# Query halves turned by a DMA instead of by TensorE in a two-layer attention kernel

## The reference, cut to what matters

```python
def l2norm(t):
    n = jnp.maximum(jnp.linalg.norm(t, axis=-1, keepdims=True), 1e-12)
    return t / n
x = x + _L0_cond_ref(x, mask_BxS_bf1, ...)
x = x + _L1_cond_ref(x, fside_16xSxS_0, mask_BxS_bk0, ...)
x = x + _L2_cond_ref(x, cond_64, ...)
x = x + _L3_cond_ref(x, cond_64, ...)
```

## Time and profile before

| | us |
|---|---|
| median of 3 runs | 1609.54 (1609.19 to 1610.14) |
| the profiled execution, its own time | 1607.64 |
| its span, first to last instruction | 1605.8 |
| the two attention layers, from the first bias step (40.5) to the last (1261.5) | 1221 |
| behind them, nearly all expert layers | 344.3 |
| mean granted TensorE clock, share of full speed | 0.988 |

### The profile page before, as it was taken

How to read it: one execution, slowest core, us unless ns; L and a number is a source line. 1 busy time by engine, 2 the same in 40 slices (tenths; PEclk the granted TensorE clock), 3 DMA queues, 4 the chain that set the end, 5 groups by cost and what they waited for, 6 DMA issues and landing times.

```text
span 1605.8 us, 45604 instructions
## 1 busy us (share of the span) xinstructions
PE 1435.0 (89%) x15700; PEld 1077.4 (67%) x15700; DVE 1394.6 (87%) x3629; ACT 1154.0 (72%) x3061; POOL 901.5 (56%) x1766
## 2 busy tenths in 40 slices
PE   4777878888999999977789999999999999999998
PEld 3555656666777777755666777777878656666665
DVE  6667888899999999977789999999999889888887
ACT  4666778888989999977788888889889633333332
POOL 6676778775756556577665354444343366622222
PEclk9899999999999999999999999999999999999999
DMA  5002211112222133012222122333333100000000
GB/s 159 18 30 72 67 48 54 62 66 74 80 87 86 55 107 118 23 48 67 54 61 80 61 74 87 97 97 107 113 116 94 38 27 21 1 1 1 14 14 27
DMA packets 67362, 100.70 MB, mean 63 GB/s; under 512 B 20330, under 2 KB 43968, under 8 KB 67136
## 3 DMA queue, kind: packets, MB, share of 16 engines
q1 hardware_dynamic: 65828, 97.12, 19.1%
q10 hardware_dynamic: 1308, 0.67, 0.2%
HBM read 91.41 MB, written 2.17 MB: 58 GB/s over the span
## 4 chain that ended last, share of the span: by engine, by line
PE 56%; DVE 22%; issue 7%; ACT 6%; POOL 4%; DVEq 0%; ACTq 0%; POOLq 0%
PE tp L1833 9%; DVE biased L1289 6%; PE sc L1696 6%; DVE p_lo L1387 6%; PE sc L1481 4%; PE sc L1483 4%; PE sc L1482 4%; PE sc L1697 4%; DVE q_a L1321 3%; PE aux L1481 3%; PE op L1481 3%; PE aux L1483 2%; PE aux L1482 2%; PE op L1483 2%; PE op L1482 2%
## 5 line engine op out<-in xcount | busy, mean ns | idle before, releaser
L1387 DVE TENSOR_TENSOR p_lo<-tp,p_hi 128x256 f16<-128x256 f32 (+3 forms) x896 | 422.0, 495 | 73.7 <-ACT p_hi L968 65.4
L1833 PE MATMUL tp<-ident,probs 128*128 128x128 f32 x2304 | 416.6, 281 | 18.7 <-DVE p_lo L1387 16.9
L968 ACT ACTIVATE p_hi<-tp 128x256 f16<-128x256 f32 (+3 forms) x896 | 384.9, 445 | 40.5 <-PE tp L1833 25.5
L868 ACT ACTIVATE probs<-biased,neg_max 128x256 f32<-128x256 f32 (+7 forms) x512 | 395.8, 773 | 17.5 <-DVE neg_max L1289 16.2
L1481 PE MATMUL op<-v_s,p_hi 128*128 128x64 f16 x2304 | 297.2, 194 | 23.7 <-DVE p_lo L1387 15.0
L1696 PE MATMUL sc<-k_a,q_a 128*128 128x512 f16 (+3 forms) x768 | 253.6, 330 | 69.0 <-DVE neg_max L1289 54.1
L1833 PEld LDWEIGHTS tp<-ident,probs 128*128 128x128 f32 x2304 | 262.7, 142 | 56.2 <-DVE p_lo L1387 44.3
L1482 PE MATMUL op<-v_s,p_hi 128*128 128x64 f16 x2304 | 296.9, 193 | 0.0
L1483 PE MATMUL op<-v_s,p_lo 128*128 128x64 f16 x2304 | 296.9, 193 | 0.0
L1481 PEld LDWEIGHTS op<-v_s,p_hi 128*128 128x128 f16 x2304 | 220.0, 99 | 41.5 <-DVE p_lo L1387 25.2
L1697 PE MATMUL sc<-k_b,q_b 128*128 128x512 f16 (+3 forms) x768 | 241.3, 328 | 0.0
(11 more groups left out here) (356 smaller groups left out, 3612.5 us busy)
## 6 DMA issues: line engine op xcount, KB each, us to landing
bias<-rel_table SPq DMA_DIRECT2D x4, 2048.0 KB, 9.1
bias<-in_fside_16xSxS SPq DMA_DIRECT2D x4, 2048.0 KB, 9.0
bias<-rel_table SPq DMA_DIRECT2D x4, 1792.0 KB, 7.3
bias<-in_fside_16xSxS SPq DMA_DIRECT2D x4, 1792.0 KB, 7.9
bias<-rel_table SPq DMA_DIRECT2D x4, 1536.0 KB, 6.1
bias<-in_fside_16xSxS SPq DMA_DIRECT2D x4, 1536.0 KB, 7.0
bias<-rel_table SPq DMA_DIRECT2D x4, 1280.0 KB, 5.9
bias<-in_fside_16xSxS SPq DMA_DIRECT2D x4, 1280.0 KB, 6.5
```

The lines of the kernel that those rows point to most:

```text
L868: ac.activation(probs[:, i % 2, 0:w], biased[:, i % 2, 0:w], ACT.Exp, bias=neg_max[:, u % 2, i % HU:i % HU + 1], scale=-1.0, accum_out=row ...
L968: ac.activation(p_hi[:, gi % 4, 0:nb * P], tp[gi % 2][:, 0:nb * P], ACT.Copy)\
L1387: ve.tensor_tensor(p_lo[:, gi % 4, 0:nb * P], tp[gi % 2][:, 0:nb * P], p_hi[:, gi % 4, 0:nb * P], ALU.subtract).then_inc(s["p_lo"], 1)
L1833: last = te.transpose(tp[gi % 2][:, jj * P:(jj + 1) * P], probs[:, n % 2, (j0 + jj) * P:(j0 + jj + 1) * P], ident[:, :])
```

## The change: queries rounded first, turned by a DMA

Queries of all 128 units are rounded to two fp16 halves while still in row layout, stored side by side per head (`q_16`: head, half, 64 numbers), and one DMA transpose per unit writes both halves, stacked on 128 partitions, into `q_a`. GpSimd's copy now goes from `q_a` to `q_b`. TensorE's two transposes, ScalarE's two copies and VectorE's two subtractions of k=3 are gone. In layer 0 the rounding stands behind the norm, at k=0 of the slot group two units ahead: ScalarE copies `q_n` from SBUF, VectorE subtracts from SBUF. In layer 1 it stands at k=1, from PSUM, in place of the copy to `q_n`. `q_n` has one buffer now. `queries_by_dma` is true for every unit, so the old branches stay in the code unused. In the diff below the two ScalarE pieces are the slots k=0 (layer 0) and k=1 (layer 1), then VectorE's, then TensorE's behind the projection.

```diff
+        q_16 = sb("q_16", [P, 2, HU, 2, DH], F16)
+        def queries_by_dma(u):
+            return u >= 0
...
+        def turn_queries(eng, u):
+            if not (u < NU and queries_by_dma(u)):
+                return
+            eng.wait_ge(s["q_low"], query_turns(u))
+            if u >= 2:
+                eng.wait_ge(s["scores"], HU * (u - 1))
+            eng.dma_start_transpose(q_a[:, u % 2, :].rearrange("p (h q) -> p h q", q=P),
+                                    q_16[:, u % 2, :, :, :].rearrange("p h e d -> p (h e d)")).then_inc(s_queries[u % 2], 16)
...
             load_bias(sp, 1)
+            turn_queries(sp, 0)
+            turn_queries(sp, 1)
             n_jobs = 3
             for g in range(2, STEPS * HG):
                 if g % HG == 0 and g <= 3 * HG:
                     write_table(sp, g // HG)
-                for u in (2 * g - 5, 2 * g - 4):
-                    turn_outputs(sp, u)
+                turn_queries(sp, 2 * g - 2)
+                turn_outputs(sp, 2 * g - 5)
+                turn_queries(sp, 2 * g - 1)
+                turn_outputs(sp, 2 * g - 4)
                 load_bias(sp, g)
-                if n_jobs < 10 and g == load_at(n_jobs) + 1:
+                if n_jobs < 10 and g == load_at(n_jobs) + (4 if n_jobs == 5 else 1):
...
             def query_copy(u):
+                if queries_by_dma(u):
+                    pool.wait_ge(s_queries[u % 2], 16 * pair_turns(u))
+                    gp.tensor_copy(q_b[0:DH, u % 2, :], q_a[0:DH, u % 2, :]).then_inc(s["q_dup"], 1)
...
+                if k == 0 and 0 <= m + 2 < U0:
+                    u = m + 2
+                    act.wait_ge(s["q_nd"], u + 1)
+                    if u >= 2:
+                        act.wait_ge(s_queries[u % 2], 16 * pair_turns(u - 2))
+                    ac.activation(q_16[:, u % 2, :, 0, :], q_n[:, 0, :].rearrange("p (h d) -> p h d", h=HU),
+                                  ACT.Copy).then_inc(s["q_high"], 1)
...
+                        ac.activation(q_16[:, u % 2, :, 0, :], first[:, 0:UW].rearrange("p (h d) -> p h d", h=HU),
+                                      ACT.Copy, scale=DH ** -0.5 / WS).then_inc(s["q_high"], 1)
...
+                if k == 1 and U0 <= m + 3 < NU:
+                    u = m + 3
+                    dve.wait_ge(s["q_high"], query_turns(u))
+                    ve.scalar_tensor_tensor(q_16[:, u % 2, :, 1, :], first[:, 0:UW].rearrange("p (h d) -> p h d", h=HU),
+                                            DH ** -0.5 / WS, q_16[:, u % 2, :, 0, :], ALU.mult, ALU.subtract)\
+                        .then_inc(s["q_low"], 1)
+                if k == 0 and 0 <= m + 2 < U0:
+                    u = m + 2
+                    dve.wait_ge(s["q_high"], query_turns(u))
+                    ve.tensor_tensor(q_16[:, u % 2, :, 1, :], q_n[:, 0, :].rearrange("p (h d) -> p h d", h=HU),
+                                     q_16[:, u % 2, :, 0, :], ALU.subtract).then_inc(s["q_low"], 1)
...
+                    if u < U0:
+                        take(False, (s["q_na"], u + 1), (s["q_sq"], u + 1))
+                    else:
+                        take(False, (s["q_high"], query_turns(u)), (s["q_low"], query_turns(u)))
```

More of the change, by code:

```diff
@@ L124, in model @@
         q_b = sb("q_b", [P, 2, HU * P], F16)
-        q_n = sb("q_n", [P, 2, UW])
+        q_n = sb("q_n", [P, 1, UW])
+        q_16 = sb("q_16", [P, 2, HU, 2, DH], F16)
         q_sq = sb("q_sq", [P, HU, DH])
@@ L247, in halves_first, with query_turns, pair_turns @@
             return u // UNITS % TILES >= TILES // 2
+        def queries_by_dma(u):
+            return u >= 0
+        def query_turns(u):
+            return sum(queries_by_dma(i) for i in range(u + 1))
+        def pair_turns(u):
+            return sum(queries_by_dma(i) for i in range(u % 2, u + 1, 2))
         def by_dma(u):
@@ L304, in model @@
                     q_proj q_sq q_ss q_nd q_na q_t q_hi q_lo q_dup wnk null_t null
-                    x_st x_rs xn xt xt_hi xt_lo xr_hi xr_lo kv kv_act kv_r kv_d kv_v k_dup kt k_hi k_lo
+                    q_high q_low x_st x_rs xn xt xt_hi xt_lo xr_hi xr_lo kv kv_act kv_r kv_d kv_v k_dup kt k_hi k_lo
                     d_null p_null denom r_den o_null o_raw o_n ot ot_hi ot_in y y_s y_acc
@@ L315, in model @@
         s_turn = sem("outputs_turned")
+        s_queries = [sem(f"queries_turned{i}") for i in range(2)]
         s_bias = [sem(f"bias_in{i}") for i in range(2)]
@@ L512, in _ @@
             for u in range(2 * STEPS * HG - 5, NU):
+                turn_queries(sp, u + 3)
                 turn_outputs(sp, u)
@@ L882, in _ @@
                     ac.activation(dst, first[:, 0:D], ACT.Copy, scale=1.0 / WS).then_inc(s["y_s"], 1)
-                if k == 3 and 0 <= m + 2 < NU:
+                if k == 3 and 0 <= m + 2 < NU and not queries_by_dma(m + 2):
                     u = m + 2
@@ L899, in _ @@
                             .then_inc(s["q_sq"], 1)
-                    ac.activation(q_n[:, u % 2, :], first[:, 0:UW], ACT.Copy, scale=1.0 if u < U0 else DH ** -0.5 / WS)\
-                        .then_inc(s["q_na"], 1)
+                    if u < U0:
+                        if u >= 1:
+                            act.wait_ge(s["q_low"], u)
+                        ac.activation(q_n[:, 0, :], first[:, 0:UW], ACT.Copy).then_inc(s["q_na"], 1)
+                    else:
+                        if query_turns(u - 2) > 0:
+                            act.wait_ge(s_queries[u % 2], 16 * pair_turns(u - 2))
+                        else:
+                            act.wait_ge(s["q_t"], u - 1)
+                        ac.activation(q_16[:, u % 2, :, 0, :], first[:, 0:UW].rearrange("p (h d) -> p h d", h=HU),
+                                      ACT.Copy, scale=DH ** -0.5 / WS).then_inc(s["q_high"], 1)
                 def small():
@@ L1682, in _ @@
                         pe.wait_ge(s["q_dup"], u + 1)
[L1683 removed]
+                        if not queries_by_dma(u):
+                            pe.wait_ge(s["q_lo"], 2 * (u + 1))
                         if u % UNITS == 0:
```

10 lines of the change are left out of this document (6 added, 4 removed).

## The result

The changed kernel took 1597.01 us (median of 4 runs, 1596.06 to 1598.01), the one before 1609.84 (4 runs, 1609.19 to 1610.56): ratio 0.992, 95% interval 0.9903 to 0.9937. That is 12.8 us faster; 29 were forecast. The span is 1593.6 us, the mean granted clock 0.976 (0.988 before).

A forecast was written before the change was run, and what follows sets the result against it. Expert layers were taken as bound by TensorE, long stages by TensorE with VectorE close, short stages by round trips between engines. 16 + 8 + 19 - 12 - 2 = 29 us gained gave 1580 us, range 1560 to 1600.

The forecast's parts named there:

- The removed work: Per unit: TensorE's two transposes (0.22 us), ScalarE's two copies (2 x 0.376), VectorE's two subtractions (2 x 0.423) go.
- Layer 1, short stages: 32 units: 29.5 us of detour on the chain, new 0.41 on VectorE returns whole; 16 us gained.
- Layer 0, short stages: 32 units: 21.4 us of detour on the chain, half of new 0.38 + 0.41 on the path; 8 us gained.
- The second rival: Layer 0: all 64 VectorE subtractions held up 0.45 us, half on the path, gaining nothing; 1595 or 1600; chance 0.15.
- Long stages: 64 units: TensorE's 0.22 us plus a third of 0.24 us bank waits each; 19 us gained.
- Table writes: Query transposes of units 6, 14, 22 land late behind write_table: 4.0, 4.0, 3.8 us; 12 lost, bounds 6 and 15.
- Bank: aux after the projection is free only once VectorE read it; up to 0.7 us x 12, taken as 2 us lost.

The follow-up runs named there:

- a: Changed kernel with the even unit's query transpose issued ahead of the table write at g = 4, 8 and 12; 1577.26 us, ratio 0.9797.
- b: Changed kernel with layer 0's queries turned by TensorE as before, layer 1's by DMA; 1589.27 us, ratio 0.9874.
- f: Kernel a with queries of layer 0's first four stages (units 0 to 31) turned by TensorE, all others by DMA; 1576.49 us, ratio 0.979.
- g: Kernel a without GpSimd's power instruction in layer 0, a constant replacing the query norm; 1563.16 us, ratio 0.9716.
- h: Control: the kernel before the change, without GpSimd's power instruction in layer 0, a constant replacing the query norm; 1602.67 us, ratio 0.9961.
- d: Changed kernel, late transposes kept, plus 24 idle TensorE transposes ahead of its wait for units 6, 14 and 22; 1591.37 us, ratio 0.9884.
- e: Kernel a plus two idle TensorE transposes at each k=3 in the first four stages; 1578.62 us, ratio 0.9811.

## Why the prediction was half right

1. **The removed work** went as told, and the operations' prices held in the median (above). GpSimd's wait for ScalarE's `q_b`, 143 us, vanished; no run prices it alone, and the stages leave no room for it.
2. **Layer 1, short stages: 16 us, measured 14.8.** Right: stages 8 to 11 by 2.4, 4.4, 4.2 and 3.7 against "about 4 each".
3. **Layer 0, short stages: 8 us, measured nothing** (+0.7 in a; with TensorE turning there, +0.5 in b and -0.5 in f). This step failed. I halved the new 0.79 us per unit and assumed that the rest of the chain stays; g and h show that the 8 us are there (7.4) only without GpSimd's power. With it, GpSimd's part of the chain doubled. The sign was in the rows: GpSimd was busy 46.8 of 66.9 us in stage 1, and `q_r` stood on the chain with 2.1%. Whether the power acts through `d_null` or through `q_n` stays open.

The second rival named the right outcome for these stages, with another cause. It had all 64 of VectorE's subtractions held up. Their median is 426 ns and their mean 554 (35.4 us for 64), against 421 and 420 for the ones with a PSUM operand. The Trainium skill ("SBUF — State Buffer", section "SBUF: two separate sides") has the exclusive port pair for two SBUF inputs beside a GpSimd instruction that reads SBUF. The trace agrees, and shows when it strikes:

```profile
480.79 0.73 POOL L747 TENSOR_TENSOR y_acc<-y_acc,y_s 128x256 f32<-128x256 f32 x1
481.05 0.75 DVE L1376 TENSOR_TENSOR q<-q_n,q 128x256 f16<-128x256 f32 x1 [0.28 <-ACT q L931]
```

GpSimd's addition had 0.47 us left when the subtraction began, and the subtraction took 0.28 longer than that. So it is with all 25 that took over 0.5 us: each lasted 0.28 us longer than the GpSimd instruction that was running when it began. The other 39 began beside none, beside one with at most 0.17 us left, or, once, beside a power. In stages 0 to 3 only 4 of 30 were held up, 1.3 us of extra time in all (2.7 in a); in stages 4 to 7 it was 20 of 32, 6.8 us. That is too little for the 8 missing us, and g, with more of it in stages 0 to 3 than a (4.6 us), is the fastest run.
4. **Long stages: 19 us, measured 16.0** (10.4 + 5.6). That is net of the bank's 2 us (point 6), so 17 is the number to set it against: within the bounds, but by errors that in part cancel. Stages 4 to 6 gave 3.9, 3.3 and 2.7, more than 2.4 each; stage 7 gave 0.6, stages 12 to 14 only 1.1 to 1.2 each. In 12 to 14 that is 0.14 per unit, and 0.22, the least that I took, with the bank's waits added back; stage 15, which has no such wait, gave 2.2, 0.27 per unit. In stage 7 TensorE's work shrank by 2.7 us and its idle time grew by 2.1, of which the bank's wait there is 0.8. Over stages 12 to 14 VectorE's wait for `p_hi` ahead of `p_lo` rose, before and after:

```profile
DVE p_lo L1387 <- ACT p_hi L968: 5.3, 20, 0.4
```
```profile
DVE p_lo L1448 <- ACT p_hi L1018: 13.2, 21, 1.6
```

The rounding at k=1, ahead of `p_hi` and `p_lo`, may return a part; no run shows that it does.
5. **Table writes: 12 us, measured 18 to 19.7**, beyond the upper bound of 15. The mechanism, the three units and the gap (4.0, 4.0, 3.8 forecast; 4.15, 4.16, 3.83 measured) were right; the term was mis-sized, because I took TensorE's gap for the cost. That GpSimd and VectorE stand still too was forecast; that the second and third place cost 1.7 and 4.1 us beyond the gap was not. TensorE ran at 1.2 GHz behind each gap, and the stages that had more time at 1.2 GHz than in a are the ones that cost more than their gap (d). I had named the clock for the bound of 5 us per place; the third place passed even that.
6. **Bank: 2 us forecast**, for twelve places. TensorE waited for `aux` to be read by VectorE at four, once each in stages 7, 12, 13 and 14. Right in size.

```profile
PE aux L1841 <- DVE q L1370: 2.8, 4, 0.8
```

By the traces 14.8 (stages 8 to 11) + 16.0 (long stages, the bank in it) - 18.6 (stages 0 to 3) = 12.2, just what the span gave up; by the medians it is 12.8. Of the 29 forecast, 16 + 19 - 2 = 33 stood against 30.8 measured, and 8 - 12 = -4 for stages 0 to 3 against -18.6. So the miss lies in those four stages: 8 us of gain that didn't come and 6 to 8 us more for the table writes, both in the same direction. 1597 lay within the range, near its slow end, only because the range reached as far as rival 2's 1600, which stood there for another reason.

## What to carry to other kernels

Look at what stands ahead of a new DMA in its issuing queue: one statement's order was worth 20 of 32 us here, more than the change gained without it. When a detour leaves a round trip between engines, ask which other list ends just behind it; here GpSimd, busy 70% of stage 1 and with 2.1% of the chain in one power, was enough for the whole gain of these stages to go. Ask not how long that list is but what stands in it ahead of the next result that somebody waits for. A long wait in the list of waits is not yet a cost: here VectorE's 51 us ahead of the subtraction only covered the wait for `p_hi` behind it, and taking them away made the kernel slower.

## What the runs showed of the hardware

- A gap of 4 us in TensorE's work, with GpSimd and VectorE idle too, cost 4.4, 5.9 and 7.9 us at the three places by the traces (19.7 us in all by the medians). Right behind the three gaps the granted clock was 1.2 GHz for 6.8, 3.4 and 6.8 us, and not at all where 24 idle transposes had filled them (d). The two stages of d with no more time at 1.2 GHz than in a cost 3.5 and 4.4 us.
- In layer 0's short stages TensorE's clock didn't show in the time: 29.5 and 20.5 us at 1.2 GHz between 40 and 320 us (a and e) gave 1577.3 and 1578.6 us.
- A VectorE subtraction of 128x256 with both inputs in SBUF took 0.41 to 0.46 us when it wasn't held up. When it began while a GpSimd instruction other than a power had 0.28 us or more left, it took that remainder plus 0.28 us, in all 25 such cases of the changed kernel, up to 1.00 us. With one input in PSUM all 64 took 0.41 to 0.43.
- Twice as many DMA packets (136990 against 67362), with the transposes among bias loads of up to 2 MB, left the landing at 2.4 us in the median, 9.7 at most (4.1 for the output transposes before). Apart from the three table writes GpSimd waited for a DMA once, 2.8 us, in the changed kernel.
